# Causal attention tiles packed into full PSUM banks for two heads, with both causal passes moved to other slots

## The chip, the cores and the metric

The kernel runs on one core of one Trainium2 chip. The metric is the device time of the program in microseconds (us). All names of engines are those of the profile: PE is TensorE (PEld its weight loads), DVE is VectorE, ACT is ScalarE, POOL is GpSimd, SP is the engine that issues the DMA transfers.

## The reference

The input is 8 batches of 512 tokens of 128 numbers. One block of four parts runs over it, each after a layer norm and with a residual. In short:

```python
x = x + attn_a(layernorm(x))   # 16 heads of 8, causal, ALiBi:
#   scores = q @ k.T / sqrt(8) + where(k <= q, -(q - k), -1e30); softmax; @ v; @ w_out.T + b_out
x = x + ffn(layernorm(x))      # (silu(x @ wg.T) * (x @ wu.T)) @ wd.T, 384 hidden
x = x + attn_b(layernorm(x))   # full 512x512 softmax of each head only to rank tokens:
#   entropy, largest weight and influence choose 51 tokens; 64 compressed ones are added;
#   then attention of all queries over these 115 keys; @ Wo
x = x + ffn(layernorm(x))
```

Only attention a is touched by the change. Its scores are needed for pairs with k <= q alone: of the 4 by 4 squares of 128 by 128 in a head, ten, of which the four on the diagonal need a mask.

## The kernel before

**Slots.** Every engine's program is written as one loop over slots. A batch has its own count `a` of slots (`own_slots`), and a new batch starts every 64 slots (`NMAIN`), so that in the steady part one slot holds the work of up to four batches at different stages. What stands in a slot is set by constants: `A1_AT` (first causal pass), `A_TMAX`, `A_ROWS`, `A2_AT` (second causal pass), `A_TURN`, `A_GATE` and so on. I call a slot by its number `a` modulo 64. In each slot one "main tile" is worked as well, from slot `a` = 96 of the first batch on: one 128x512 tile of attention b. PE writes its scores one slot ahead (L1223) into a ring of three banks, DVE takes the maximum (L1045), ACT the exponential and its log sum (L811, L814), POOL a threshold (L680), DVE the entropy sum (L955, one slot later); PE adds four tiles' influence every fourth slot (L1231). Engines run their own program in order and wait only for semaphores.

**The first causal pass** (`causal_scores`, L1159 to L1164; `causal_maxima`, L916) finds the row maxima of each head. A head has three tiles (`CAUSAL`): query block 3 with 512 keys; blocks 0 and 2 with 128 and 384; block 1 with 256. Each block is one product, and then its diagonal square gets the mask by two more products of 64 columns each (L1162, L1164). The tiles alternate between banks 3 and 4, two a slot: 48 tiles, slots 0 to 23. DVE reduces each block one slot after it was written. Then the maxima are transposed (`A_TMAX` = 25, L1170), split into bf16 parts by ACT and POOL, and go through DRAM into rows of the query stack (`A_ROWS` = 28).

**The second pass** (`causal_minus_max`, L1181 to L1185) makes the scores again, keys on partitions, with the maximum taken off, again three tiles a head (`TILES`, widths 512, 512 and 256), two a slot, slots 32 to 55. ACT takes the exponential one slot later (L798) into `pT`. Heads go in gangs of four; when all four have a chunk, `weigh` (L1199) multiplies it with the values into bank 5. At the end of a gang ACT copies bank 5 out (`leave`, L781), PE transposes it into bank 7 (`turn_heads`, L1206, slots 40, 46, 52, 58) and DVE normalises (`norm_four`).

**Bank 7** is used by everything that is not one of these passes: a user claims it when the one before has been read (`claim`, by order of slots). In the slots that matter here it serves the feed-forward parts: of attention a's batch in slots 2 to 10 (gates in 2, 3, 4, silu in 5, ups in 6, 7, 8, down in 10), and of the batch three before in slots 43 to 51 (gates 43, 44, 45, silu 46, ups 48, 49, 50, down 51). ACT reads a gate in its own slot; DVE reads an up one slot later (`hidden`, L949).

**Layer norms** on POOL (L645, L652) stand in slots 24, 63, 12 and 35.

## Time and profile before

| | us |
|---|---|
| median of 3 runs | 1942.5 (1940.46 to 1942.92) |
| profiled execution | 1941.34, span 1939.2 |
| PE, DVE, ACT, POOL busy | 1524.0, 1224.2, 1006.8, 385.6 |
| first and last main tile (L1045) start | 245.3 and 1789.5 |
| one period (64 slots) in the middle | 209.6 |
| granted TensorE clock, mean | 0.687 of full speed |

Busy time is a union of the recorded times; the end of a matmul is modelled, so PE's is not what PE could not do without. The core is at work on five to six stages at once, so a share over the whole span says little; the period in the middle, cut where the change cuts, says more.

### The profile page before, as it was taken

To read this page: it belongs to the slowest core of one execution; us is meant where nothing else is said; L and a number is where in the kernel's file an instruction comes from. 1 tells how busy PE (TensorE), PEld (TensorE's weight loads), DVE (VectorE), ACT (ScalarE), POOL (GpSimd) and SP (SyncE) were. 2 spreads that over 40 slices of the span, in tenths; PEclk is the share of its full clock that TensorE was granted. 3 is DMA by queue.
4 is the path that set the end of the run, shared out by engine and by line. 5 is a ranking of instruction groups with operands and counts; after the bars stand their busy time and mean duration, and the time that the engine had idled before them with its cause. 6 is when DMAs were issued, how large, how long until landed. Compare 5 with 4: busy or idle time off the path is not lost.

```text
span 1939.2 us, 26667 instructions
## 1 busy us (share of the span) xinstructions
PE 1524.0 (79%) x8717; PEld 690.2 (36%) x8717; DVE 1224.2 (63%) x3259; ACT 1006.8 (52%) x2542; POOL 385.6 (20%) x900
## 2 busy tenths in 40 slices
PE   1687787878788888898889888788888878678655
PEld 1333443343344343353334343344334332321312
DVE  1503568866976577756876587757786667787211
ACT  1052276466556655656556655665565757546122
POOL 3110311320133011410133022310221012110100
PEclk9555588667766677668667786777666867665555
DMA  2110111121012110112012110221011002100000
GB/s 59 31 36 17 44 52 17 37 60 23 19 41 60 23 22 14 47 44 44 3 49 52 23 24 12 73 36 27 13 35 34 12 8 49 28 13 12 15 10 6
DMA packets 65626, 59.28 MB, mean 31 GB/s; under 512 B 11936, under 2 KB 63184, under 8 KB 65488
## 3 DMA queue, kind: packets, MB, share of 16 engines
q1 hardware_dynamic: 65488, 57.58, 13.3%
q8 instruction: 69, 1.13, 0.3%
q14 instruction: 69, 0.57, 0.1%
...
## 4 chain that ended last, share of the span: by engine, by line
PE 50%; DVE 23%; ACT 13%; issue 6%; POOL 5%; DMA 1%; ACTq 0%; SPq 0%; POOLq 0%; DVEq 0%
PE bank L1231 7%; PE bank L1271 7%; DVE nm L916 6%; DVE junk L955 5%; ACT setup L811 4%; PE bank L1223 4%; PE bank L1199 3%; PE bank L1254 3%; PE bank L1181 3%; PE bank L1159 3%; ACT pT L798 3%; DVE nmB L1045 3%; POOL xn L652 3%; DVE nm L923 2%; PE bank L1390 2%
## 5 line engine op out<-in xcount | busy, mean ns | idle before, releaser
L811 ACT ACTIVATE setup<-bank,nmB 128x512 f32<-128x512 f32 x512 | 350.3, 684 | 291.7 <-DVE nmB L1045 291.6
L955 DVE SCALAR_TENSOR_TENSOR junk<-bank,thr,setup 128x512 f32<-128x512 f32 x512 | 379.4, 741 | 84.8 <-POOL thr L680 81.5
L1045 DVE TENSOR_REDUCE nmB<-bank 128x1 f32<-128x512 f32 x512 | 351.2, 686 | 97.5 <-PE bank L1223 97.0
L1223 PE MATMUL bank<-k_stacks,q_stacks 48*128 48x512 bf16 x512 | 248.6, 487 | 135.5 <-DVE junk L955 133.1
L680 POOL TENSOR_TENSOR thr<-lnZ,nmB 128x1 f32<-128x1 f32 x512 | 96.5, 189 | 1223.5 <-ACT lnZ L814 1223.2
L916 DVE TENSOR_REDUCE nm<-bank 128x1 f32<-128x512 f32 (+3 forms) x512 | 223.7, 483 | 141.4 <-PE bank L1164 138.8
L798 ACT ACTIVATE pT<-bank 128x512 f32<-128x512 f32 (+1 forms) x384 | 184.1, 520 | 174.4 <-PE bank L1185 172.1
L1159 PE MATMUL bank<-k_stacks,q_stacks 52*128 52x512 bf16 (+3 forms) x512 | 177.1, 393 | 38.7 <-DMA k_stacks<-part_dram 17.7
L1231 PE MATMUL bank<-setup,rz 128*1 128x512 f32 x1024 | 196.6, 852 | 0.0
L1181 PE MATMUL bank<-q_stacks,k_stacks 55*128 55x384 bf16 (+3 forms) x512 | 159.2, 359 | 38.3 <-ACT pT L798 32.8
L1223 PEld LDWEIGHTS bank<-k_stacks,q_stacks 48*128 48x128 bf16 x512 | 49.5, 97 | 321.7 <-DVE junk L955 247.4
L1159 PEld LDWEIGHTS bank<-k_stacks,q_stacks 52*128 52x128 bf16 x512 | 54.5, 107 | 189.0 <-issue 121.8
L893 ACT ACTIVATE p<-bank 115x512 f32<-115x512 f32 x128 | 75.3, 588 | 87.3 <-PE bank L1390 87.0
L1199 PE MATMUL bank<-pT,vA 128*9 128x512 f32 (+3 forms) x1024 | 115.0, 554 | 1.0 <-ACT pT L798 1.0
L1162 PE MATMUL bank<-maskr,maskw 64*128 64x64 bf16 x512 | 114.6, 232 | 0.0
L1390 PE MATMUL bank<-s_stacks,kcst 51*115 51x512 bf16 x128 | 75.5, 590 | 49.4 <-ACT p L893 19.5
L814 ACT ACTIVATE lnZ<-Z 128x1 f32<-128x1 f32 x512 | 103.9, 203 | 16.2
L1164 PE MATMUL bank<-maskr,maskw 64*128 64x64 bf16 x512 | 109.0, 219 | 0.0
L1271 PE MATMUL bank<-xnT,wuT 128*128 128x512 f32 x96 | 81.8, 947 | 31.6 <-DVE gated L949 30.3
L1181 PEld LDWEIGHTS bank<-q_stacks,k_stacks 55*128 55x128 bf16 x512 | 52.7, 103 | 145.4 <-issue 81.5
L1183 PE MATMUL bank<-maskr,maskw 64*128 64x64 bf16 x512 | 104.2, 218 | 0.0
L811 ACT ACTIVATION_READ_ACCUMULATOR setup<-bank,nmB 128x1 f32 x512 | 102.2, 200 | 0.0
...
## 6 DMA issues: line engine op xcount, KB each, us to landing
...
q_stacks<-part_dram SPq DMA_DIRECT2D x192, 64.0 KB
k_stacks<-part_dram SPq DMA_DIRECT2D x192, 64.0 KB
...
```

The costliest lines, as they stand in the source:

```text
L798: act.activation(pT[h % HPQ][:, c * T:c * T + WIDTH[c]], bank[3 + u % 2][:, 0:WIDTH[c]], ACT.Exp).then_inc(s_free[3 + u % 2], 1)
L811: act.activation(E[:, n % NE, :], RING[n % RN][:, :], ACT.Exp, bias=nmB[mb % 2][:, h, t:t + 1], accum_out=Z[mb % 2][:, h, t:t + 1]).then_i ...
L916: last = dve.tensor_reduce(nm[0][:, t, h:h + 1], bank[k][:, at:at + (t + 1) * P], AX_X, ALU.max, negate=True)
L955: dve.scalar_tensor_tensor(out=junk[:, :], in0=RING[n % RN][:, :], scalar=thr[mb % 2][:, h, t:t + 1], in1=E[:, n % NE, :], op0=ALU.max, op ...
L1045: dve.tensor_reduce(nmB[mb % 2][:, h, t:t + 1], RING[n % RN][:, :], AX_X, ALU.max, negate=True).then_inc(s_bm, 1)
L1159: pe.matmul(bank[k][:, at:at + (t + 1) * P], qst[0][0:A_SC, h, t * P:(t + 1) * P], kst[0][0:A_SC, h, 0:(t + 1) * P], start=True, stop=True)
L1162: pe.matmul(bank[k][:, at + t * P:at + t * P + HF], maskw[:, 2, :], maskr[:, 2, :], start=False, stop=True, skip_group_check=True)
L1181: pe.matmul(bank[k][:, at:at + w], kst[0][0:A_MX, h, j * P:(j + 1) * P], qst[0][0:A_MX, h, j * P:T], start=True, stop=True)
L1199: last = pe.matmul(bank[5][QROWS * j:QROWS * j + HD + 1, k * P:T], vA[:, k, HPQ * g + j, :], pT[j][:, c * T + at:c * T + at + T - k * P], ...
L1223: pe.matmul(RING[n % RN][:, :], qst[1][0:B_SC, h, t * P:(t + 1) * P], kst[1][0:B_SC, h, :], start=True, stop=True).then_inc(s_bs, 1)
L1231: last = pe.matmul(INFL[QROWS * t:QROWS * t + 1, :], rz[mb % 2][:, h, t:t + 1], E[:, (NT * h + t) % NE, :], start=(h == 0), stop=(h == H - 1))
L1271: pe.matmul(bank[7][:, :], w, xnT[u][:, :], start=True, stop=True).then_inc(s_full[7], 1)
```

## The change

Both passes get tiles that fill a bank. In the first pass two heads share five tiles (`FIRST_TILES`): the four diagonal squares of one head, those of the other, blocks 3 and 1 below the diagonal (384 and 128 keys) of each, and block 2 (256) of both. The four diagonal squares are four products of 128 columns; their masks are two products of 4x64 columns. DVE takes the maxima of the diagonal squares in one instruction with four results, those of the other blocks into a second tile `nml`, and joins both with one minimum of negated maxima (a new instruction and a new semaphore `s_nm`). In the second pass the chunks of 256 of two heads share a tile, so that a gang has ten tiles and not twelve; squares of one bank share their masks. `pT` becomes one tensor, so that one exponential can write two heads.

A pass is 20 slots and not 24: the first in slots 8 to 27 (before 0 to 23), the second in 36 to 55 (before 32 to 55). What follows a pass moves with it: maxima transposed in 29 (25), rows in 32 (28), `weigh` in 38, 40, 41 and every five slots, turns in 43, 48, 53, 58 (40, 46, 52, 58). The next batch's preparation is two slots later (statistics 25, norm 26, transposes 28, q and k 30 and 31).

```diff
+    FIRST_TILES = (((0, None),), ((1, None),), ((0, 3), (0, 1)), ((1, 3), (1, 1)), ((0, 2), (1, 2)))
+    NF = len(FIRST_TILES)
     TILES = (((0, 0),), ((1, 0), (3, T - P)), ((2, 0),))
     WIDTH = (T, T, T - 2 * P)
-    CAUSAL = (((3, 0),), ((0, 0), (2, P)), ((1, 0),))
+    SHARE = (1, 1, 2)
...
+        pT = sb("pT", [P, 4, sum(WIDTH)])
         p2 = [sb(f"p2_{i}", [P, T]) for i in range(4)]
         ov = sb("ov", [P, T])
...
         INFL_LAG = 5
+        N1 = NF * H2
+        GANG = [(c, j) for c in range(3) for j in range(0, HPQ, SHARE[c])]
+        G2 = len(GANG)
+        N2 = G2 * NG
+        CHUNK_END = [max(i for i, (e, _) in enumerate(GANG) if e == c) for c in range(3)]
         LEAD = 1
-        FIRST = 44
-        X_LOAD = -44
-        P_STATS = -41
-        P_LN = -40
-        P_TURN = -38
-        P_Q, P_K = -36, -35
-        P_STORE = -30
-        P_HALF = (-20, -8)
+        FIRST = 42
+        X_LOAD = -42
+        P_STATS = -39
+        P_LN = -38
+        P_TURN = -36
+        P_Q, P_K = -34, -33
+        P_STORE = -28
+        P_HALF = (-17, -7)
         P_V = -4
-        A1_AT = 0
+        A1_AT = 8
         XBO = 19
-        A_TMAX = 25
-        A_ROWS = 28
-        A2_AT = 32
-        A_TURN = tuple(A2_AT + 8 + 6 * g for g in range(NG))
+        A_TMAX = 29
+        A_ROWS = 32
+        A2_AT = 36
+        A_TURN = tuple(A2_AT + 7 + 5 * g for g in range(NG))
+        WEIGH = tuple(A2_AT + 5 * g + (2, 4, 5)[c] for g in range(NG) for c in range(3))
         A_OUT = 60
         A_PROJ = 61
         A_LN = 63
...
-            for u in range(3 * H):
+            for u in range(N1):
                 use(3 + u % 2, z + A1_AT + u // 2, "a1", b, u)
+            for u in range(N2):
                 use(3 + u % 2, z + A2_AT + u // 2, "a2", b, u)
             use(3, z + A_TMAX, "tmax", b)
             for g in range(NG):
-                use(5, z + A2_AT + 2 + 6 * g, "weigh", b, g)
+                use(5, z + WEIGH[3 * g], "weigh", b, g)
                 use(7, z + A_TURN[g], "turn", b, g)
             use(7, z + A_OUT, "out", 0, b)
             use(7, z + A_PROJ, "proj", 0, b)
...
-            return HPQ * (u // (3 * HPQ)) + u % HPQ, u // HPQ % 3
+            c, j = GANG[u % G2]
+            return u // G2, c, range(j, j + SHARE[c])
         def own_slots(g):
...
+                        for u in range(N2):
                             if a == A2_AT + u // 2 + 1:
-                                h, c = gang_tile(u)
-                                if 3 * NG * b + u // HPQ > 2:
-                                    act.wait_ge(s_pv[0], 3 * NG * b + u // HPQ - 2)
+                                gang, c, js = gang_tile(u)
+                                if NG * b + gang:
+                                    act.wait_ge(s_pv[0], 3 * (NG * b + gang - 1) + c + 1)
                                 act.wait_ge(s_full[3 + u % 2], turn[3 + u % 2]["a2", b, u] + 1)
-                                act.activation(pT[h % HPQ][:, c * T:c * T + WIDTH[c]], bank[3 + u % 2][:, 0:WIDTH[c]],
+                                act.activation(pT[:, js[0]:js[0] + len(js), c * T:c * T + WIDTH[c]],
+                                               bank[3 + u % 2][:, :].rearrange("p (j q) -> p j q", j=len(js)),
                                                ACT.Exp).then_inc(s_free[3 + u % 2], 1)
                         for j in range(NG):
...
                 def causal_maxima(b, u):
-                    h, k = u // 3, 3 + u % 2
+                    k, blocks = 3 + u % 2, FIRST_TILES[u % NF]
+                    h = 2 * (u // NF) + blocks[0][0]
                     dve.wait_ge(s_full[k], turn[k]["a1", b, u] + 1)
-                    for t, at in CAUSAL[u % 3]:
-                        last = dve.tensor_reduce(nm[0][:, t, h:h + 1], bank[k][:, at:at + (t + 1) * P], AX_X, ALU.max,
-                                                 negate=True)
+                    if blocks[0][1] is None:
+                        last = dve.tensor_reduce(nm[0][:, :, h], bank[k][:, :].rearrange("p (t k) -> p t k", t=NT), AX_X,
+                                                 ALU.max, negate=True)
+                    elif blocks[0][1] == blocks[1][1]:
+                        last = dve.tensor_reduce(nml[:, 2, h:h + 2], bank[k][:, :].rearrange("p (j k) -> p j k", j=2), AX_X,
+                                                 ALU.max, negate=True)
+                    else:
+                        dve.tensor_reduce(nml[:, 3, h:h + 1], bank[k][:, 0:3 * P], AX_X, ALU.max, negate=True)
+                        last = dve.tensor_reduce(nml[:, 1, h:h + 1], bank[k][:, 3 * P:T], AX_X, ALU.max, negate=True)
                     last.then_inc(s_free[k], 1)
                 def small_maxima(b, h):
...
+                        for u in range(N1):
                             if a == A1_AT + u // 2 + 1:
                                 causal_maxima(b, u)
+                        if a == A_TMAX - 1:
+                            dve.wait_ge(s_free[3], turn[3]["a1", b, N1 - 2] + 1)
+                            dve.wait_ge(s_free[4], turn[4]["a1", b, N1 - 1] + 1)
+                            dve.tensor_tensor(nm[0][:, 1:NT, :], nm[0][:, 1:NT, :], nml[:, 1:NT, :], ALU.min
+                                              ).then_inc(s_nm, 1)
                         for h in range(H):
                             if a == S1_AT + h // 2 + 1:
                                 small_maxima(b, h)
...
                 def causal_scores(b, u):
-                    h, k = u // 3, 3 + u % 2
+                    k = 3 + u % 2
                     claim(k, "a1", b, u)
-                    if u in (0, 3 * H2):
-                        pe.wait_ge(s_stack[0][u // (3 * H2)], 2 * NPAIR * DMA * (b + 1))
-                    for t, at in CAUSAL[u % 3]:
-                        pe.matmul(bank[k][:, at:at + (t + 1) * P],
-                                  qst[0][0:A_SC, h, t * P:(t + 1) * P], kst[0][0:A_SC, h, 0:(t + 1) * P],
-                                  start=True, stop=True)
-                        pe.matmul(bank[k][:, at + t * P:at + t * P + HF], maskw[:, 2, :], maskr[:, 2, :],
-                                  start=False, stop=True, skip_group_check=True)
-                        last = pe.matmul(bank[k][:, at + t * P + HF:at + (t + 1) * P], maskw[:, 3, :], maskr[:, 3, :],
-                                         start=False, stop=True, skip_group_check=True)
+                    if u in (0, N1 // 2):
+                        pe.wait_ge(s_stack[0][2 * u // N1], 2 * NPAIR * DMA * (b + 1))
+                    at = 0
+                    for j, t in FIRST_TILES[u % NF]:
+                        h = 2 * (u // NF) + j
+                        if t is None:
+                            for t in range(NT):
+                                here = slice(t * P, (t + 1) * P)
+                                pe.matmul(bank[k][:, here], qst[0][0:A_SC, h, here], kst[0][0:A_SC, h, here],
+                                          start=(t == 0), stop=True, skip_group_check=(t > 0))
+                            halves = bank[k][:, :].rearrange("p (t c k) -> p t c k", t=NT, c=2)
+                            for c in range(2):
+                                last = pe.matmul(halves[:, :, c, :], maskw[:, 2 + c, :],
+                                                 maskr[:, 2 + c:3 + c, :].broadcast_to([HF, NT, HF]), start=False,
+                                                 stop=True, skip_group_check=True)
+                        else:
+                            last = pe.matmul(bank[k][:, at:at + t * P], qst[0][0:A_SC, h, t * P:(t + 1) * P],
+                                             kst[0][0:A_SC, h, 0:t * P], start=True, stop=True)
+                            at += t * P
                     last.then_inc(s_full[k], 1)
                 def transpose_max(s, ps):
...
                 def causal_minus_max(b, u):
-                    h, c = gang_tile(u)
+                    g, c, js = gang_tile(u)
                     k = 3 + u % 2
                     claim(k, "a2", b, u)
                     if u == 0:
                         pe.wait_ge(s_mrow[0], DMA * (b + 1))
-                    for j, at in TILES[c]:
-                        w = T - j * P
-                        pe.matmul(bank[k][:, at:at + w], kst[0][0:A_MX, h, j * P:(j + 1) * P],
-                                  qst[0][0:A_MX, h, j * P:T], start=True, stop=True)
-                        pe.matmul(bank[k][:, at:at + HF], maskw[:, 0, :], maskr[:, 0, :],
-                                  start=False, stop=True, skip_group_check=True)
-                        last = pe.matmul(bank[k][:, at + HF:at + P], maskw[:, 1, :], maskr[:, 1, :],
-                                         start=False, stop=True, skip_group_check=True)
+                    squares = []
+                    for i, head in enumerate(js):
+                        h = HPQ * g + head
+                        for j, at in TILES[c]:
+                            w, first = T - j * P, i * WIDTH[c] + at
+                            pe.matmul(bank[k][:, first:first + w], kst[0][0:A_MX, h, j * P:(j + 1) * P],
+                                      qst[0][0:A_MX, h, j * P:T], start=not squares, stop=True,
+                                      skip_group_check=bool(squares))
+                            squares.append(first // P)
+                    blocks = bank[k][:, :].rearrange("p (t c q) -> p t c q", t=NT, c=2)
+                    step = squares[-1] - squares[0] or 1
+                    for half in range(2):
+                        last = pe.matmul(blocks[:, squares[0]:squares[-1] + 1:step, half, :], maskw[:, half, :],
+                                         maskr[:, half:half + 1, :].broadcast_to([HF, len(squares), HF]), start=False,
+                                         stop=True, skip_group_check=True)
                     last.then_inc(s_full[k], 1)
                 def weigh(b, w):
                     g, c = w // 3, w % 3
-                    u = HPQ * w + HPQ - 1
-                    pe.wait_ge(s_free[3 + u % 2], turn[3 + u % 2]["a2", b, u] + 1)
+                    for u in (g * G2 + CHUNK_END[c] - 1, g * G2 + CHUNK_END[c]):
+                        pe.wait_ge(s_free[3 + u % 2], turn[3 + u % 2]["a2", b, u] + 1)
                     if c == 0:
                         claim(5, "weigh", b, g)
                     if w == 0:
...
-                            pe.wait_ge(s_free[4], turn[4]["a1", b, 3 * H - 1] + 1)
+                            pe.wait_ge(s_nm, b + 1)
                             transpose_max(0, bank[3]).then_inc(s_full[3], 1)
                         for j in range(NG):
                             if a == A_TURN[j]:
```


PE, the first tiles of the first causal pass at the program's start: before, one head is twelve products in three tiles.

```order
L1159 MATMUL bank3<-k_stacks,q_stacks 128x512
L1162 MATMUL bank3<-maskr,maskw 128x64
L1164 MATMUL bank3<-maskr,maskw 128x64
L1159 MATMUL bank4<-k_stacks,q_stacks 128x128
L1162 MATMUL bank4<-maskr,maskw 128x64
L1164 MATMUL bank4<-maskr,maskw 128x64
L1159 MATMUL bank4<-k_stacks,q_stacks 128x384
L1162 MATMUL bank4<-maskr,maskw 128x64
L1164 MATMUL bank4<-maskr,maskw 128x64
L1159 MATMUL bank3<-k_stacks,q_stacks 128x256
L1162 MATMUL bank3<-maskr,maskw 128x64
L1164 MATMUL bank3<-maskr,maskw 128x64
```


Now two heads are five tiles (the four products of a row with x4 are the diagonal squares of one head).

```order
L1192 MATMUL bank3<-k_stacks,q_stacks 128x128 x4
L1196 MATMUL bank3<-maskr,maskw 128x4x64 x2
L1192 MATMUL bank4<-k_stacks,q_stacks 128x128 x4
L1196 MATMUL bank4<-maskr,maskw 128x4x64 x2
L1200 MATMUL bank3<-k_stacks,q_stacks 128x384
L1200 MATMUL bank3<-k_stacks,q_stacks 128x128
L1200 MATMUL bank4<-k_stacks,q_stacks 128x384
L1200 MATMUL bank4<-k_stacks,q_stacks 128x128
L1200 MATMUL bank3<-k_stacks,q_stacks 128x256 x2
```


The masks went from eight products a head to two, the blocks from four to seven; the columns are the same.

PE, where a feed-forward part and the second pass meet (batches three and later): before, slot 45 with the last gate, and the start of slot 46. L1223 is the main tile's product, L1271 a gate, L1231 the influence, L1206 the turn.

```order
L1223 MATMUL bank1<-k_stacks,q_stacks 128x512
L1271 MATMUL bank7<-xnT1,wgT 128x512
L1231 MATMUL bank6<-setup,rz0 1x512 x4
L1181 MATMUL bank3<-q_stacks,k_stacks 128x512
L1183 MATMUL bank3<-maskr,maskw 128x64
L1185 MATMUL bank3<-maskr,maskw 128x64
L1181 MATMUL bank4<-q_stacks,k_stacks 128x512
L1183 MATMUL bank4<-maskr,maskw 128x64
L1185 MATMUL bank4<-maskr,maskw 128x64
L1223 MATMUL bank2<-k_stacks,q_stacks 128x512
L1206 MATMUL bank7<-identf,ov 128x128 x4
```


Now, slot 43 with the first gate, and the start of slot 44. L1268 is the main tile's product, L1316 a gate, L1251 the turn, L1221 and L1229 are the second pass, L1244 is `weigh`.

```order
L1268 MATMUL bank1<-k_stacks,q_stacks 128x512
L1316 MATMUL bank7<-xnT1,wgT 128x512
L1251 MATMUL bank7<-identf,ov 128x128 x4
L1221 MATMUL bank3<-q_stacks,k_stacks 128x384
L1221 MATMUL bank3<-q_stacks,k_stacks 128x128
L1229 MATMUL bank3<-maskr,maskw 128x2x64 x2
L1221 MATMUL bank4<-q_stacks,k_stacks 128x384
L1221 MATMUL bank4<-q_stacks,k_stacks 128x128
L1229 MATMUL bank4<-maskr,maskw 128x2x64 x2
L1244 MATMUL bank5<-pT,vA 9x512 x4
L1268 MATMUL bank2<-k_stacks,q_stacks 128x512
L1316 MATMUL bank7<-xnT1,wgT 128x512
```


The turn used to stand in the slot after the last gate. It now follows the first gate directly, and both write bank 7; in slot 48 it follows the first up (wuT) in the same way.

## Rows read from the trace of the kernel before

**Rows 1.** The page: busy time by engine, and the chain that ended last, by engine

```profile
PE 1524.0 (79%) x8717; PEld 690.2 (36%) x8717; DVE 1224.2 (63%) x3259; ACT 1006.8 (52%) x2542; POOL 385.6 (20%) x900
...
PE 50%; DVE 23%; ACT 13%; issue 6%; POOL 5%; DMA 1%; ACTq 0%; SPq 0%; POOLq 0%; DVEq 0%
```

**Rows 2.** Stretches of one period: length, busy PE, PEld, DVE, ACT, POOL, PEclk, DMA

```profile
1148.00:1170.20 22.20, 18.55 (x99) 7.07 (x99) 19.95 (x51) 15.73 (x34) 7.52 (x15) 0.81 0.02 5
1170.20:1227.50 57.30, 47.57 (x270) 21.52 (x269) 45.16 (x120) 28.67 (x73) 15.40 (x33) 0.65 0.14 42
1227.50:1239.00 11.50, 9.22 (x42) 3.25 (x42) 9.04 (x26) 6.33 (x17) 5.94 (x10) 0.69 0.00 0
1239.00:1250.00 11.00, 9.23 (x26) 1.65 (x26) 6.36 (x18) 10.16 (x26) 3.78 (x7) 0.69 0.06 17
1040.40:1057.50 17.10, 16.74 (x113) 10.26 (x112) 11.33 (x38) 9.98 (x26) 3.97 (x10) 0.69 0.53 113
1057.50:1125.80 68.30, 58.95 (x421) 27.36 (x418) 38.77 (x112) 43.55 (x112) 8.20 (x26) 0.78 0.13 24
1125.80:1148.00 22.20, 16.18 (x120) 9.07 (x120) 21.17 (x58) 9.70 (x31) 2.03 (x11) 0.80 0.21 37
```

**Rows 3.** Groups of instructions by form: a mask product (busy us, mean ns)

```profile
L1162 PE MATMUL bank<-maskr,maskw 64*128 64x64 bf16 x512 | 114.6, 232 | 0.0
```

**Rows 4.** Timeline of PE (start us, us): mask products, clock low, then full

```profile
1149.64 0.26 PE L1162 MATMUL bank<-maskr,maskw 64*128 64x64 bf16 x1
1149.71 0.24 PE L1164 MATMUL bank<-maskr,maskw 64*128 64x64 bf16 x1
...
1163.98 0.19 PE L1162 MATMUL bank<-maskr,maskw 64*128 64x64 bf16 x1
1164.01 0.19 PE L1164 MATMUL bank<-maskr,maskw 64*128 64x64 bf16 x1
```

**Rows 5.** Timeline of DVE: statistics; a full tile, three smaller reductions, what follows

```profile
1225.70 0.86 DVE L905 BATCH_NORM_STATS2 st<-x 128x6 f32<-128x128 f32 x4
1226.60 0.38 DVE L909 BATCH_NORM_AGGREGATE mv<-st 128x2 f32<-128x6 f32 x4
...
1227.54 0.68 DVE L1045 TENSOR_REDUCE nmB<-bank 128x1 f32<-128x512 f32 x1
1228.14 1.07 DVE L916 TENSOR_REDUCE nm<-bank 128x1 f32<-128x128 f32 x3
1229.13 0.16 DVE L1058 RECIPROCAL rz<-Z 128x4 f32<-128x4 f32 x1
```

**Rows 6.** Timelines of POOL, PE, DVE and ACT: slots 0 to 5 of the period

```profile
1148.96 3.13 POOL L652 TENSOR_SCALAR xn<-x,mv,rstd 128x128 f32<-128x128 f32 x4
...
1155.33 0.60 PE L1223 MATMUL bank<-k_stacks,q_stacks 48*128 48x512 bf16 x1
...
1157.41 0.69 DVE L1045 TENSOR_REDUCE nmB<-bank 128x1 f32<-128x512 f32 x1
...
1165.31 1.48 ACT L785 ACTIVATE gated<-gated 128x1536 f32<-128x1536 f32 x1
```

**Rows 7.** Timelines: bank 7 in slots 43, 46 and 48 (PE, ACT, DVE)

```profile
1087.51 1.13 PE L1271 MATMUL bank<-xnT,wgT 128*128 128x512 f32 x2
...
1094.59 0.66 PE L1206 MATMUL bank<-identf,ov 128*128 128x128 f32 x4
...
1102.66 2.07 PE L1271 MATMUL bank<-xnT,wuT 128*128 128x512 f32 x2
...
1088.68 0.60 ACT L727 ACTIVATE gated<-bank 128x512 f32<-128x512 f32 x1 [0.44 <-PE bank L1271]
...
1104.77 0.69 DVE L949 TENSOR_TENSOR gated<-bank,gated 128x512 f32<-128x512 f32 x1 [0.44 <-PE bank L1271]
```

**Rows 8.** Stretches of the start, same columns: the first two passes alone

```profile
55.00:90.40 35.40, 29.44 (x192) 16.12 (x190) 27.64 (x69) 0.00 (x0) 0.00 (x0) 0.50 0.14 22
105.00:158.20 53.20, 49.43 (x330) 21.25 (x330) 1.92 (x8) 26.09 (x52) 1.11 (x2) 0.50 0.16 37
```

14 lines of the change are left out of this document (7 added, 7 removed).

## The prediction

> **What bounds the kernel now.** I read the page first. PE is recorded busy for 1524.0 of 1939.2 us and is half of the chain that ended last, with DVE at 23% [rows 1]. That does not say which pass waits for what, so I cut one period in the middle at the starts of main tiles, where the change cuts [rows 2]. In order these are slots 0 to 7, 8 to 23, 24 to 27, 28 to 31, then (from the start of the same period) 32 to 35, 36 to 55 and 56 to 63. The reader is to compare each length with the busy time of each engine. Slots 0 to 7, which hold a feed-forward part beside the first pass, are DVE's (19.95 of 22.20). Slots 8 to 23 are nobody's alone (PE 47.57, DVE 45.16 of 57.30). Slots 28 to 31 are ACT's (10.16 of 11.00). Slots 32 to 35 are PE's (16.74 of 17.10). Slots 36 to 55 are mostly PE's (58.95 of 68.30), and 56 to 63 DVE's. So both passes run in stretches where they cost time, and the question is what their work costs in the new place against the old one.
>
> **The masks.** 2048 mask products become 896: 8 to 2 a head in the first pass, 32 to 20 a gang in the second. The page gives one of them 232 ns [rows 3]. That is its way through the array, not what it costs: the next product starts 0.07 us after it at the low clock and 0.03 us at the full one [rows 4]. 64 columns at 1.2 and 2.4 GHz are 0.053 and 0.027, so PE pays for columns, and the columns are the same before and after (1792 a head and pass). What goes is the rest of 0.003 to 0.017 a product: 1152 fewer masks and 384 more block products are 768 instructions, at most 13 us of PE over the whole program if all are at the upper end, some 4 us at 0.005. PE is the limit in little more than half of the time and PE's other gaps swallow part of it: I take 0 to 5 us, and none in the sum.
>
> **DVE.** A full tile keeps the next instruction away for 0.60 us. Three reductions of 768 columns together take 0.99 [rows 5]. Two equations give 0.067 + 0.00104 a column. One reduction of seven (two heads had eight) is 0.067 x 64 = 4.3 us saved over eight batches, less eight joins of 48 numbers (estimated 0.12 each). For a slot it gives the old load 853 columns and 2.67 reductions, 1.065 us; the new load is 1024 and 2.8, 1.25 us. The Trainium skill ("VectorE: DVE Perf Modes", the TRN2 errata) has a fixed 120 cycles for a PSUM source, 0.125 us at 0.96 GHz. By it the saving would be 8 us; the rows show half of that from start to start.
>
> **ACT.** A gang had eight full and four half tiles, and has ten full ones: the same columns, two instructions fewer. I give that nothing, as ACT's own queue bounds few slots.
>
> **The first pass moves from slots 0-23 to 8-27.** Six batches do this beside main tiles.
> *Slots 0 to 7.* POOL's norm ends at 1152.09, whatever DVE does, so slots 63 to 1 give back nothing. The next main product on PE is at 1155.33, and DVE could take its maximum at about 1155.9, but takes it at 1157.41, after the first pass's tile [rows 6]: 1.5 back. From there three gates at 1.85 each (PE 1.13, ACT 0.60 to read it [rows 7], 0.12 of hand-over, an estimate) bring silu's activation to about 1162.5 where it is at 1165.31 now [rows 6]: 2.8 back. The first `hidden` behind it no longer stands behind a slot's reductions and their main tile's work on DVE (1.25 and 1.27): up to 2.4 more. Together at most some 5.2, if the clock is full for all of it. The stretch's granted clock is 0.81 [rows 2]. If the gates run at the low one, each costs 2.07 [rows 7] and 2.5 is left. I take 4.0.
> *Slots 8 to 23.* DVE gets 16 x 0.185 = 2.96, less slot 8 (no tile is ready yet, 1.06) and less the statistics of the next batch, which leave for slot 25 (1.1 [rows 5]): 0.8. PE gets 0.133 head a slot, 16 x 0.133 x 1792 columns, 3.2 us at 1.2 GHz and 2.4 at the granted 0.65. Between these: 1.5 lost.
> *Slots 24 to 27.* DVE has 9.04 of 11.50. It gets 4 x 1.25, less 1.06 of slot 24, plus 1.1: 14.1. That is 2.6 over the present length before any stall, and 5.1 if all of the present 2.5 of idle stays. 3.0 lost.
> *Slots 28 to 31.* The transposes and bf16 parts of the maxima come in (three ACT copies like the one of 0.60 in [rows 7], on 10.16 of 11.00; two copies of the next batch's parts go out), and q now follows the maxima by one slot where it had three. 0 to 2.5 lost, 1.3 taken.
> Net 1.8 lost a batch, 10.8 for six.
>
> **The second pass moves from 32-55 to 36-55.** Slots 32 to 35 lose eight tiles of PE work, 5632 columns, 4.7 us at 1.2 GHz, and one `weigh` of 1.8; at the granted 0.69 that is 4.7, and PE is the limit there. ACT and DVE then stand near: 4.3 gained. Slots 36 to 55 get the same 6.5 us of low-clock work back; at 0.78 it is 4.2 us, of which 86% is where PE is busy, and slots that are ACT's pay for 8 more half tiles. 3.5 lost. Net 0.8 gained, seven batches: 5.6.
>
> **A wait that is new.** The turn needs bank 7. In slot 43 it now stands behind the first gate, and so waits until ACT has read it; in slot 48 behind the first up, until DVE has. Today PE goes on with second-pass tiles in that time. The gate starts at 1087.51 and is read by 1089.2; the up starts at 1102.66, ends at 1104.73 and is read by 1105.4 [rows 7]. PE stands 0.6 to 0.8 each time, with the tiles and the `weigh` of the slot queued behind, and ACT's exponentials behind these. 1.6 a batch for the five batches where both meet: 8.0. Bound: 0 if PE would wait for ACT in these slots anyway, 3 a batch if ACT falls a slot behind. The turn itself (0.66) only moves.
>
> **The start.** Batch 0's passes run alone. The first takes 35.40 for 16 heads, of which DVE is busy 27.64, 0.48 a head of waiting for three tiles; two and a half tiles and half a reduction less give back 0.11 a head, 1.8. The second takes 53.2 for four gangs at clock 0.50 [rows 8]; its 12288 columns a gang fill 41.0 of them at 1.2 GHz (a float32 column of `weigh` counted four times, an estimate from the 2.07 of the up in [rows 7]), so 12 hand-overs cost 3.0 a gang, and ten give back 0.5, 2.0 in all. Batch 1's first pass has its first eight slots hidden under a feed-forward part today and will have three: 2.5 lost. Sum 1.3 gained.
>
> **Sum.** 10.8 - 5.6 + 8.0 - 1.3 = 11.9 us more, on the profiled 1941.34, which is 1.2 below the median of 1942.5: 1953.2, or 1954.4 against the median. I keep back 2 for the masks and the DVE instruction: 1952.
>
> **Rivals.**
> *The dense slots swallow the work (faster, 0.31).* Slots 8 to 31 have 79.8 us against 60.6 of DVE, and 36 to 55 have 9 us without PE. If the added work falls into those gaps, the lower ends hold: -5.2 + 0.8 + 2.6 + 0 = -1.8 for six, -4.7 + 2.0 = -2.7 for seven, and half of the bank-7 wait: -10.8 - 18.9 + 4 - 1.3 = -27, 1915. Half of that is 1928. It decides if slots 24 to 27 grow by under 3 and slots 0 to 7 shrink by over 4.
> *The clock (slower, 0.10).* In 1148.0 to 1170.2 the granted share is 0.81. Without the first pass PE has gaps there: if it stays at 1.2 GHz through the three gates and three ups, these cost 0.94 more each, 5.6 a batch, and 12 + 34 gives up to 1985; half of it is 1970.
> *The masks are on the path (faster, 0.05).* If each product waited for the one before to leave the array, a removed mask would be worth its recorded 0.232 [rows 3]: 1152 x 0.232 = 267 us off PE, half of it on the chain [rows 1], 1808. The starts in [rows 4] speak against it. The Trainium skill ("TensorE: Matmul & The Clock Gate", single matmul latency) gives an isolated product (219 + N)/1.2 ns, 236 for 64 columns; by that rule alone the saving would be this rival's.
> *Nothing (0.12).* The terms have both signs and may cancel: 1939 to 1946.
>
> **How the numbers follow.** The forecast, slower by the sum, has 0.42, its own range is 1947 to 1970. A measurement of this kernel tells 0.2% (4 us) from no change. Slower has 0.40 + 0.10 = 0.50, the same 0.12 + 0.02 of the forecast = 0.14, faster 0.31 + 0.05 = 0.36. The range 1915 to 1978 leaves out the masks' case, the ends of the first two rivals, together under 0.2.
>
> **What would show it.** Right: slots 0 to 7 take about 18 us in the new trace, slots 24 to 27 above 14 with DVE full, 32 to 35 about 13; PE idles before the turn (L1251) behind an ACT or DVE read of bank 7 some ten times by 0.6 to 0.8; mask products start 0.21 us apart at the low clock where they are 4x64. PE's recorded busy time falls by far more than the span moves. Wrong: slots 8 to 31 no longer than now, a PE clock well off 0.687, or the maxima rows late at slot 36 (SP now issues the next half stack right behind them).

## The result, and the profile after

| | before | after |
|---|---|---|
| median of 18 runs each, us | 1941.24 (1935.53 to 1952.88) | 1929.83 (1910.79 to 1943.08) |
| span and granted clock of the profiled execution | 1939.2, 0.687 | 1928.7, 0.692 |

The ratio is 0.9926, with a 95% interval of 0.9901 to 0.9951. The change makes the kernel faster, by 11 us, where I forecast 12 us slower. 1929.83 lies inside the range of 1915 to 1978, on the other side of the kernel before.

The page of after, busy time by engine and the chain by engine (as [rows 1] of before):

```profile
PE 1487.1 (77%) x7949; PEld 652.0 (34%) x7949; DVE 1223.3 (63%) x3203; ACT 1001.2 (52%) x2478; POOL 389.4 (20%) x900
...
PE 50%; DVE 22%; ACT 15%; issue 7%; POOL 3%; DMA 2%; SPq 0%; ACTq 0%; POOLq 0%; DVEq 0%
```

768 products fewer, as worked out. DVE's time has not moved: seven reductions for two heads are a little longer each than eight were. The chain's shares are nearly the same too.

The middle period of after, cut at the same slots as [rows 2] (0 to 7, 8 to 23, 24 to 27, 28 to 31, then from the start of that period 32 to 35, 36 to 55, 56 to 63). Columns: length, busy PE, PEld, DVE, ACT, POOL, granted clock, DMA:

```profile
1135.20:1155.30 20.10, 14.55 (x42) 3.74 (x42) 12.81 (x32) 15.45 (x34) 7.54 (x15) 0.75 0.02 5
1155.30:1209.60 54.30, 45.08 (x251) 20.60 (x252) 45.59 (x112) 28.19 (x73) 15.39 (x33) 0.69 0.17 41
1209.60:1223.90 14.30, 11.82 (x63) 4.25 (x61) 13.97 (x42) 6.93 (x19) 4.87 (x10) 0.62 0.08 15
1223.90:1234.00 10.10, 8.75 (x36) 2.31 (x34) 7.55 (x21) 7.94 (x20) 1.83 (x6) 0.63 0.00 0
1022.40:1038.60 16.20, 13.32 (x78) 8.52 (x78) 12.05 (x34) 10.31 (x26) 10.42 (x15) 0.73 0.39 102
1038.60:1110.60 72.00, 59.93 (x388) 27.44 (x388) 38.97 (x112) 44.76 (x109) 5.71 (x23) 0.78 0.17 31
1110.60:1135.20 24.60, 19.40 (x141) 10.52 (x140) 21.37 (x58) 10.63 (x31) 2.02 (x11) 0.73 0.20 33
```

Length against the forecast for it:

| slots | before | after | difference | forecast |
|---|---|---|---|---|
| 0 to 7 | 22.2 | 20.1 | -2.1 | -4.0 |
| 8 to 23 | 57.3 | 54.3 | -3.0 | +1.5 |
| 24 to 27 | 11.5 | 14.3 | +2.8 | +3.0 |
| 28 to 31 | 11.0 | 10.1 | -0.9 | +1.3 |
| 32 to 35 | 17.1 | 16.2 | -0.9 | -4.3 |
| 36 to 55 | 68.3 | 72.0 | +3.7 | +3.5, and 1.6 of the wait |
| 56 to 63 | 22.2 | 24.6 | +2.4 | 0 |

This period grew by 2.0. But it was one of the shortest of before: four of its periods in a row, counted from slot 0, take 212.9, 217.7, 211.3 and 209.1 (the period of the table, cut at slot 32, takes 209.6). So I take four whole periods of each (first row before, then after), with the columns as above:

```profile
506.10:1357.10 851.00, 718.37 (x4353) 329.59 (x4352) 607.50 (x1627) 499.92 (x1264) 187.27 (x433) 0.72 0.15 34
```

```profile
499.80:1346.80 847.00, 691.70 (x3969) 309.43 (x3968) 609.09 (x1599) 497.12 (x1232) 191.17 (x433) 0.73 0.16 34
```

Four periods gain 4.0 us, 1.0 each. Of their stretches, slots 8 to 23 change most: their mean is 58.3 us before, at clock 0.63, and 54.4 after, at 0.69. Length times clock, which is microseconds of full clock, is 36.8 before and 37.5 after: the columns that moved in are there, and the stretch is shorter all the same, because the clock is higher.

The start gains more. The first main tile stands at 245.3 before and at 230.2 after, 15.1 earlier; but where the four periods begin (506.1 and 499.8) only 6.3 of it is left. What follows the four periods takes 582.1 and 581.9. So the 10.5 us between the two spans are 6.3 and 4.0, and 0.2 behind. The start in after: the first pass alone, and the second pass alone in two parts (as [rows 8]):

```profile
55.20:88.00 32.80, 28.22 (x140) 12.65 (x138) 27.25 (x62) 0.00 (x0) 3.22 (x5) 0.50 0.13 22
101.20:125.00 23.80, 23.33 (x140) 9.44 (x141) 0.55 (x2) 12.77 (x23) 0.00 (x0) 0.50 0.13 44
125.00:138.80 13.80, 12.64 (x126) 6.10 (x122) 1.10 (x4) 10.53 (x20) 0.00 (x0) 0.99 0.26 41
```

From first to last exponential the second pass took 50.0 before, all at clock 0.50, and takes 37.6. The last third now runs at the full clock.

**The view that orders the rest.** The granted clock has two levels, 1.2 GHz (0.5) and 2.4 GHz (1.0), and a mean between them is a share of both. If PE always had work, the span times the mean granted clock would be the work itself in microseconds of full clock, whatever the clock did; a wait adds to it. PE is recorded busy for 77 to 79% of the span, so the product counts work and idle time together. The table has the mean of span x clock over the executions of each kernel, without six that took over 1.5% more than the fastest of their kernel (one each of the change, first_at_4, prep_new, second_alone, before_shared and after_two; that of prep_new took 2639.06 us):

| kernel | executions | span, mean | clock, mean | product |
|---|---|---|---|---|
| before | 93 | 1939.5 | 0.6878 | 1334 |
| the change | 21 | 1924.3 | 0.6921 | 1332 |
| places_old | 12 | 1949.7 | 0.6821 | 1330 |
| first_alone | 12 | 1942.0 | 0.6882 | 1336 |
| second_alone | 11 | 1937.1 | 0.6916 | 1340 |
| prep_new | 9 | 1948.5 | 0.6874 | 1340 |
| first_at_4 | 9 | 1931.7 | 0.6957 | 1344 |
| first_unpacked_late | 12 | 1934.2 | 0.6913 | 1337 |
| turn_apart, turn_again | 10 | 1925.7 | 0.6867 | 1322 |
| first_masks_pairs | 10 | 1926.0 | 0.6909 | 1331 |
| first_masks_apart | 4 | 1963.0 | 0.6790 | 1333 |
| masks_apart | 6 | 1967.2 | 0.6817 | 1341 |
| before_shared | 10 | 1931.4 | 0.6919 | 1336 |
| before_two | 4 | 679.8 | 0.5932 | 403 |
| after_two | 4 | 664.8 | 0.6042 | 402 |

Before and the change have nearly the same product, and so have their periods: the four above take 153.3 and 153.7 us of full clock each. The change is faster by about what its clock is higher: 0.6% of clock, 0.8% of time. Within one kernel, too, the quick executions are those with the higher clock (correlation -0.81 over the 93 of before, -0.86 over the 21 of the change). This says where the time went, and not what raised the clock.

### The profile page after: what moved, and what is told of

Same layout as the page of the kernel before. It is cut to its first block, busy times and chain, and to the rows that moved or that the text cites. A ratio compares the mean times of both kernels' runs of the same rounds, so it can differ in the third digit from the quotient of the medians.

```text
span 1928.7 us, 25028 instructions
## 1 busy us (share of the span) xinstructions
PE 1487.1 (77%) x7949; PEld 652.0 (34%) x7949; DVE 1223.3 (63%) x3203; ACT 1001.2 (52%) x2478; POOL 389.4 (20%) x900
## 4 chain that ended last, share of the span: by engine, by line
PE 50%; DVE 22%; ACT 15%; issue 7%; POOL 3%; DMA 2%; SPq 0%; ACTq 0%; POOLq 0%; DVEq 0%
PE bank L1276 8%; PE bank L1316 7%; DVE junk L978 5%; ACT setup L827 4%; PE bank L1268 4%; PE bank L1244 3%; PE bank L1221 3%; PE bank L1299 3%; DVE nm L946 3%; ACT pT L813 2%; DVE nmB L1068 2%; DVE nm L933 2%; PE bank L1259 2%; PE bank L1251 2%; PE bank L1200 2%
## 5 line engine op out<-in xcount | busy, mean ns | idle before, releaser
L1268 PE MATMUL bank<-k_stacks,q_stacks 48*128 48x512 bf16 x512 | 254.5, 499 | 151.8 <-DVE junk L978 150.1
L813 ACT ACTIVATE pT<-bank 128x512 f32<-128x512 f32 x320 | 174.3, 590 | 133.5 <-PE bank L1229 132.1
L1268 PEld LDWEIGHTS bank<-k_stacks,q_stacks 48*128 48x128 bf16 x512 | 49.9, 98 | 384.2 <-DVE junk L978 285.3
L1221 PE MATMUL bank<-q_stacks,k_stacks 55*128 55x384 bf16 (+3 forms) x512 | 138.9, 346 | 36.6 <-ACT pT L813 30.7
L933 DVE TENSOR_REDUCE nm<-bank 128x4 f32<-128x512 f32 x128 | 86.5, 687 | 65.8 <-PE bank L1196 65.8
L1200 PE MATMUL bank<-k_stacks,q_stacks 52*128 52x384 bf16 (+2 forms) x384 | 96.0, 364 | 12.9 <-DVE nm L933 9.6
L1244 PE MATMUL bank<-pT,vA 128*9 128x512 f32 (+3 forms) x1024 | 104.9, 511 | 0.2 <-ACT pT L813 0.2
L1316 PE MATMUL bank<-xnT,wuT 128*128 128x512 f32 x96 | 83.0, 961 | 25.8 <-DVE gated L972 23.8
L667 POOL TENSOR_SCALAR xn<-x,mv,rstd 128x128 f32<-128x128 f32 x128 | 100.1, 794 | 3.3
L1229 PE MATMUL bank<-maskr,maskw 64*128 64x128 bf16 (+1 forms) x640 | 91.4, 227 | 0.0
L1192 PE MATMUL bank<-k_stacks,q_stacks 52*128 52x128 bf16 x512 | 68.4, 275 | 29.3 <-DMA k_stacks<-part_dram 17.3
L956 DVE RECIPROCAL rzo<-bank 128x16 f32<-128x16 f32 x64 | 15.7, 245 | 113.0 <-PE bank L1251 113.0
L946 DVE TENSOR_REDUCE nm<-bank 128x4 f32<-128x460 f32 x128 | 74.9, 629 | 16.2 <-PE bank L1310 15.8
```

Source lines behind the costliest of these rows:

```text
L813: act.activation(pT[:, js[0]:js[0] + len(js), c * T:c * T + WIDTH[c]], bank[3 + u % 2][:, :].rearrange("p (j q) -> p j q", j=len(js)), ACT ...
L933: last = dve.tensor_reduce(nm[0][:, :, h], bank[k][:, :].rearrange("p (t k) -> p t k", t=NT), AX_X, ALU.max, negate=True)
L946: dve.tensor_reduce(nm[1][:, :, h], bank[k][:, 0:NT * NK].rearrange("p (t k) -> p t k", t=NT), AX_X, ALU.max, negate=True).then_inc(s_free ...
L1200: last = pe.matmul(bank[k][:, at:at + t * P], qst[0][0:A_SC, h, t * P:(t + 1) * P], kst[0][0:A_SC, h, 0:t * P], start=True, stop=True)
L1221: pe.matmul(bank[k][:, first:first + w], kst[0][0:A_MX, h, j * P:(j + 1) * P], qst[0][0:A_MX, h, j * P:T], start=not squares, stop=True, s ...
L1244: last = pe.matmul(bank[5][QROWS * j:QROWS * j + HD + 1, k * P:T], vA[:, k, HPQ * g + j, :], pT[:, j, c * T + at:c * T + at + T - k * P], ...
```

## The experiments

### Which part gains: packing, or the places

```diff
 # places_old: the change, with
-A1_AT, A_TMAX, A_ROWS, A2_AT = 8, 29, 32, 36    # and P_*, FIRST of the change
+A1_AT, A_TMAX, A_ROWS, A2_AT = 4, 25, 28, 32    # and P_*, FIRST of before
 # first_alone: first pass packed, slots 4 to 23; second pass and preparation as before
 # second_alone: second pass packed, slots 36 to 55; first pass as before, slots 0 to 23
```

> All tiles packed as in the change, but every stage near its old slot: the first pass in slots 4 to 23, the maxima at 25, the second pass in 32 to 51, the next batch's preparation as before. If the gain comes of the packing alone (fewer hand-overs, shorter passes), this is as fast as the change, some 1925 to 1932. If it comes of where the passes stand (first pass out of the feed-forward slots 0 to 7), half of slots 0 to 7 is loaded again and this is 5 to 15 us slower than the change, 1935 to 1945. The turns in 39, 44, 49, 54 meet gates and ups in two slots here too.

> Only the first causal pass is packed (20 slots, 4 to 23); the second is the old one in 32 to 55. If the steady gain is the first pass's (slots 0 to 15 were 5.4 us shorter a period in the changed trace, the second pass's slots 5 us longer), this is faster than the change: 1905 to 1925. If the gain is that of the second pass at the start (full clock for half of it), this is near the kernel before, 1935 to 1942.

> Only the second causal pass is packed (36 to 55); the first is the old one in 0 to 23. If the second pass costs in the steady part (about 5 us a period in the two traces), this is slower than the kernel before, 1945 to 1975, less what the start gives. If the start's second pass at the full clock is the gain, this is 1925 to 1935.

Measured: places_old 1952.59 us (12 runs), ratio 1.0045 [1.0022, 1.0068]; first_alone 1945.13 (12), 1.0005 [0.9983, 1.0027]; second_alone 1944.28 (12), 0.9987 [0.9962, 1.0012]. Packing at the old places loses, and neither pass alone gains. Tiles and places together do. The expectations did less well: places_old is over 7 us above both of its cases, and first_alone 3 us above "near the kernel before". For second_alone the first case holds: four of its periods take 861.3 us for 851.0 before, and the time stands at the low end of 1945 to 1975.

### Where the new places count

```diff
 # first_unpacked_late: the change, first pass with the three tiles of before, slots 4 to 27
 # first_at_4: the change, with
-A1_AT = 8
+A1_AT = 4
 # prep_new: places_old, with the preparation (P_*, FIRST) of the change
```

> The change, but with the old three tiles a head in the first pass, which stands in slots 4 to 27 (the second pass packed in 36 to 55, all else as in the change). If the steady gain comes of the first pass's end being later and its work out of the feed-forward slots, half of those slots is loaded again: slots 0 to 15 take some 50 us in a period, between the 47.6 of the change and the 53.0 of before, and the time is 1935 to 1942. If it came of fewer, fuller tiles, slots 8 to 27 are longer here as well and the time is above 1942. If neither matters, 1930.

> The change, with the first pass alone four slots earlier (slots 4 to 23 in place of 8 to 27), so that its first four slots stand beside the feed-forward products of slots 0 to 7; maxima, rows, second pass and preparation stay. Theory that the second pass's place and not the first's made the packed kernel with old places slow (there slots 32 to 63 took 118.4 us a period against 112.7 in the change, slots 0 to 31 only 100.2 against 98.8): 1.4 us a period more, 1936 to 1942 us. Rival, that the first pass must keep off the feed-forward slots: most of the 22.8 us between the two, 1945 to 1952 us. Second rival: its place doesn't count, 1928 to 1932 us.

> The packed tiles with both passes and the maxima at their old places (first pass 4 to 23, second pass 32 to 51), and the preparation of the next batch at its new ones; so it stands between places_old (1952.6 us, preparation old as well) and first_at_4 (1934.7 us, second pass at 36). Theory that the second pass's place counts, in whose stretch places_old took 118.4 us a period against 112.7: 1948 to 1956 us. Rival, that the preparation's place counts (its q and k products and transposes stood beside the last first-pass slots): 1933 to 1940 us.

Measured: first_unpacked_late 1934.67 (12 runs), 0.9971 [0.9949, 0.9993]; first_at_4 1934.73 (10), 0.9979 [0.9950, 1.0008]; prep_new 1948.27 (10), 1.0055 [1.0031, 1.0079]. With the tiles packed, the 22.8 us between old and new places are 4.3 for the preparation (1952.6 to 1948.3), 13.5 for the second pass at 36 in place of 32, the maxima moving with it (to 1934.7), and 4.9 for the first pass at 8 in place of 4 (to 1929.8). The first is within its error, the last is about as large as its error, and the middle one is well clear of it. Its sign is that of the clock: prep_new has 0.6874 and first_at_4 0.6957, at products of 1340 and 1344. Of the expectations, that of prep_new holds. first_at_4 lies between two of its cases.

first_unpacked_late has the old first pass with its 1024 masks of 64 columns, and still gains about 6 of the 11 us. So packing the first pass is not all of the gain, once the passes stand later. Its time and its slots 0 to 15 (48.1 and 49.6 us in turn) are close to what its first case had (1935 us or more, some 50).

### The new wait on bank 7

```diff
-A_TURN = tuple(A2_AT + 7 + 5 * g for g in range(NG))   # 43, 48, 53, 58
+A_TURN = (46, 52, 53, 58)
+A_LEAVE = tuple(A2_AT + 6 + 5 * g for g in range(NG))  # ACT's copy stays in its slot
```

> The change with the copy out of bank 5 kept where it is and the turns in slots 46, 52, 53, 58, so that no turn stands behind a gate or an up in its own slot. If the new wait for bank 7 costs the 1.6 us a batch that was forecast, in five batches, this is 8 us faster than the change, about 1922. If PE would have waited for ACT there anyway, it is the same within 3 us.

> The change with the turns at slots 46, 52, 53 and 58 and the leaves where they were, a second time. Theory that it takes 2 us a period out of slots 40 to 55 whatever the clock does (span times clock in slots 40 to 55 42.9 us there against 44.9 in the change), so that it lies 8 to 16 us under the change at the same start: 1915 to 1922 us, with a profile under 1915 us if its start gets the full clock. Rival, that the clock gives back what the wait had cost: 1925 to 1931 us again.

What the turn's products wait for, in the change, and then in turn_apart (idle time of PE before them in us, and times; weight loads left out):

```profile
its engine sat idle before it (us, times) until:
  ACT gated L742: 11.2, 5
  ACT ov L796: 6.5, 14
  DVE gated L972: 5.0, 5
```

```profile
its engine sat idle before it (us, times) until:
  ACT ov L797: 7.1, 17
  DVE o L959: 0.6, 1
```

The rows for the gate and the up (L742, L972) are gone. They were 2.2 us a batch for the gate and 1.0 for the up, in five batches. Slots 40 to 55 of the middle period, the change and then turn_again:

```profile
1053.80:1110.60 56.80, 48.41 (x320) 21.23 (x320) 27.28 (x65) 36.37 (x88) 3.56 (x17) 0.79 0.12 24
```

```profile
1062.30:1115.40 53.10, 47.98 (x320) 20.81 (x320) 27.01 (x65) 36.24 (x88) 3.55 (x17) 0.81 0.13 26
```

3.7 us a period, in both profiles of this version. Yet its times are 1927.74 (6 runs, ratio 0.9921 [0.9891, 0.9951]) and 1929.73 (4 runs, 0.9945 [0.9929, 0.9961]), those of the change. Its product is 10 lower, 1322, and its clock also, 0.687 for 0.692. turn_apart is not the 8 us faster that the wait should have been worth, and within 3 us of the change. Of the expectation for the second run the rival holds, in the time. The traces show where the gain is lost again, and it is not in the periods. Four whole periods of turn_apart, the same length as in turn_again:

```profile
517.50:1350.20 832.70, 689.91 (x3969) 307.75 (x3968) 608.51 (x1597) 496.88 (x1232) 191.92 (x433) 0.73 0.16 35
```

They are 14.3 us shorter than the 847.0 of the change, but they begin at 517.5 and 515.5 where those of the change begin at 499.8. The first batch's second pass ran at clock 0.54 there and at 0.68 in the change, and the slots 40 to 55 just before the four periods took 45.8 and 45.9 us at 0.66 and 0.67 where the change has 37.1 at 0.91. Why this version gets less clock there is not shown.

### The masks

```diff
 # masks_apart: both passes; first_masks_apart: first pass alone
-for c in range(2):
-    last = pe.matmul(halves[:, :, c, :], maskw[:, 2 + c, :], maskr[:, 2 + c:3 + c, :].broadcast_to([HF, NT, HF]), ...)
+for t in range(NT):
+    for c in range(2):
+        last = pe.matmul(halves[:, t, c, :], maskw[:, 2 + c, :], maskr[:, 2 + c, :], ...)
 # first_masks_pairs: halves[:, t:t + 2, c, :], two squares in a product
 # before_shared: before, its tiles and places kept; where a bank holds two squares, both
 # blocks first and then two mask products of 128 columns in place of four of 64
```

> The change with the masks not shared: every diagonal square gets its two products of 64 columns again (2048 mask products, not 896), the tiles and slots as in the change. If a mask product costs its columns (0.03 to 0.07 us from start to start), this is within 5 us of the change, 1927 to 1936. If it costs the recorded 0.23 us on the path, this is 60 us or more slower, above 1990.

> The change, with the mask products of the first pass's diagonal squares alone issued one by one (1024 of 64 columns where the change has 256 of 256 columns); the second pass keeps its 640 shared ones. Theory that the unshared masks cost granted clock in the stretch where the first pass runs: with all masks apart, slots 8 to 23 of a period took 30.5 and 29.1 us at a granted clock of 0.61 and 0.62, where the change takes 27.5 and 26.8 at 0.69, while the 64-column products start 53 ns and the 256-column ones 213 ns apart, the same time for a column. So nearly the whole 39 us should stand here: 1960 to 1972 us, ratio 1.010 to 1.016 against before, slots 8 to 31 about 6 us a period longer than in the change, and slots 32 to 63 as in the change. Rival, a fixed price of each further product (39 us over 1152 products, 34 ns each): 768 more products here, 1956 us, and starts further apart than 53 ns. Second rival, that the second pass's masks are what counts: within 5 us of the change, 1930 to 1935 us.

> The change with the first pass's mask products for two squares at a time: 512 of 128 columns, where the change has 256 of 256 and the kernel with them apart 1024 of 64; the columns are the same in all three. Theory that the granted clock falls with the count of short products in the first pass's stretch: a third of the way from 1930 to 1963 us, 1937 to 1945 us, with a clock of 0.65 to 0.68 in slots 8 to 23. Rival, a step as soon as the products are shorter than 256 columns: 1955 to 1965 us. Second rival, a step only at 64 columns: 1928 to 1933 us.

> The kernel before, its tiles, banks and places unchanged; only where a bank holds two diagonal squares (one tile of three in each pass) both blocks are computed first and their masks issued together, 128 columns each: 1024 products of 64 columns and 512 of 128 in place of 2048 of 64. Theory that 64-column masks hold the granted clock down in the kernel before as in the packed one (34 us for 1024 such products in the first pass against 256 or 512 longer ones): half of them gone, 1922 to 1933 us, ratio 0.990 to 0.996, with a clock over 0.65 in slots 8 to 23. Rival, that the price stands only where the squares of a whole head follow one another, as in the packed first pass: within 3 us of before, 1938 to 1944 us.

| | mask products and their columns | us | ratio to before |
|---|---|---|---|
| masks_apart | 2048 of 64 | 1969.10 (6 runs) | 1.0137 [1.0106, 1.0168] |
| first_masks_apart | first pass 1024 of 64 | 1963.43 (4) | 1.0129 [1.0079, 1.0178] |
| first_masks_pairs | first pass 512 of 128 | 1930.27 (10) | 0.9935 [0.9905, 0.9965] |
| before_shared | 1024 of 64, 512 of 128 | 1940.23 (11) | 0.9960 [0.9930, 0.9990] |

masks_apart lies between its two cases. Splitting the first pass's masks into 64 columns costs 34 us, as first_masks_apart had it; splitting them into 128 costs nothing, the second rival of first_masks_pairs. A fixed price for each product is out, as the 256 further products of the pairs would then have cost 11 us. The products themselves are no dearer either. A head's masks on PE at the low and at the full clock (start, us), masks_apart and then the change:

```profile
1193.76 0.63 PE L1197 MATMUL bank<-maskr,maskw 64*128 64x64 bf16 x8
...
1204.08 0.40 PE L1197 MATMUL bank<-maskr,maskw 64*128 64x64 bf16 x8
```

```profile
1159.07 0.63 PE L1196 MATMUL bank<-maskr,maskw 64*128 64x256 bf16 x2
...
1194.00 0.38 PE L1196 MATMUL bank<-maskr,maskw 64*128 64x256 bf16 x2
```

Eight products or two, 0.63 at the low clock and 0.40 or 0.38 at the full one. What differs is the clock that is granted around them. Slots 8 to 15 and 16 to 23 of one period, first_masks_apart, first_masks_pairs, and the change in a second profile (below):

```profile
1169.20:1199.60 30.40, 26.81 (x162) 13.29 (x162) 23.17 (x62) 12.18 (x32) 5.93 (x15) 0.61 0.06 18
1199.60:1228.60 29.00, 24.86 (x168) 11.73 (x168) 22.56 (x53) 16.01 (x41) 9.54 (x18) 0.62 0.25 56
```

```profile
1162.90:1190.50 27.60, 23.54 (x138) 10.75 (x138) 23.07 (x60) 12.18 (x32) 5.90 (x15) 0.69 0.07 20
1190.50:1214.40 23.90, 19.54 (x140) 9.31 (x140) 22.42 (x53) 15.76 (x41) 9.53 (x18) 0.79 0.30 64
```

```profile
1139.90:1167.40 27.50, 23.32 (x126) 10.23 (x126) 23.02 (x60) 12.18 (x32) 5.94 (x15) 0.69 0.07 20
1167.40:1191.30 23.90, 19.35 (x126) 8.79 (x126) 22.42 (x53) 15.76 (x41) 9.56 (x18) 0.79 0.30 65
```

30.4 x 0.61 is 18.5 and 27.5 x 0.69 is 19.0: no more work in microseconds of full clock, only a lower clock. The Trainium skill ("TensorE: Matmul & The Clock Gate", back-to-back issue gap) gives a start-to-start gap of the columns at the clock, plus 2.5 ns at the full one. The traces agree for a product: 64-column masks of masks_apart start 53 ns apart at the low clock and 28 or 29 at the full one, 256-column masks of the change 213 and 113. By that rule the 1152 products of masks_apart would cost under 3 us in all, an estimate; 39 are measured.

Nor do 64-column masks hold the clock down wherever they stand. first_unpacked_late has as many of them in its first pass as first_masks_apart, in the old tiles, and takes 1934.67 us; its slots 8 to 15 and 16 to 23 had the clock 0.70 and 0.79 in two of four periods (0.67 and 0.62 in the other two). So the 34 us are the price of these masks in the packed first pass.

In the kernel before the price shows in some executions only. before_shared lies 0.4% under it, near the edge of what its interval can tell, and its median missed the expected 1922 to 1933. But all but one of its times fall into two groups, five of 1921 to 1931 (clock 0.694 to 0.697) and five of 1940 to 1943 (0.688 to 0.689), and none of the 93 executions of before is under 1934.33. Its profiled execution took 1925.49. Four of its periods:

```profile
511.70:1344.50 832.80, 695.71 (x4096) 312.63 (x4096) 607.06 (x1627) 498.19 (x1264) 187.14 (x433) 0.74 0.16 35
```

That is 18.2 us less than the 851.0 of before, and in two of the four periods slots 8 to 15 and 16 to 23 have the clock 0.68 and 0.70, as its theory had it. So longer masks alone, with no packed tile and no pass moved, can give as much as the whole change, in half of the executions. What decides which execution gets it is open.

### Start or steady part

```diff
 # before_two, after_two: before and the change, with
+B = 2
 # after_again: the change itself once more
```

> The kernel before, for the first two batches alone (the other six outputs are not written): the start, two periods and the end. With the start's second pass at the low clock in every execution its times should lie close together, some 650 to 700 us, spread under 5.

> The change for the first two batches alone, to be read against the kernel before for two. If the start's gain is the clock rising in the second pass in some executions, its times spread by 10 us or more and the median is 5 to 12 us below. If the start gains by its fewer hand-overs alone, it is 1 to 4 us below with a small spread. If all of the gain is in the steady periods, it is the same.

> The change itself once more, for a second profile of it. Theory that the start's stretch of full clock (the second pass of the first batch 37.6 us, of it 12.3 and 7.7 us a gang at the low and at the full clock) comes in only some of its executions, and that a time goes with the share of the clock that was granted: a profile near the median (1927 to 1933 us) with this pass at 37 to 43 or at 45 us, whichever, and span times mean clock at 1330 to 1336 us, as in the first profile (1928.7 x 0.692 = 1334.7) and in before (1939.2 x 0.687 = 1332.2). Rival, that the start is always as in the first profile: 37 to 38 us again and the first main tile at 230 us.

before_two and after_two compute two of the eight batches and leave the other six outputs unwritten. They took 680.15 us (4 runs, 679.80 to 685.87) and 667.57 us (5 runs, 663.31 to 681.52). So two batches show a gain of 12.6, as large as eight do, and their product is nearly the same too (403 and 402). That speaks for the start as the source of the gain in the median, but does not settle it: the profiles of before and of the change with eight batches keep 6.3 us of the start, and the second profile of the change, below, gains more in its periods. The spread of before_two is 6.1, three of its four times lying within 0.5 of each other; that of after_two is 18, with one time of 681.52.

after_again took 1922.36 (4 runs), 0.9892 [0.9857, 0.9927]; its profiled execution is the fastest of all, span 1906.6 at clock 0.701. Its start is that of the first profile, as the rival had it: second pass 37.7 us, first main tile at 231.2. Its four periods take 833.3 for 847.0:

```profile
494.70:1328.00 833.30, 681.45 (x3969) 303.03 (x3968) 608.17 (x1599) 495.90 (x1232) 191.87 (x433) 0.74 0.17 35
```

The difference lies in slots 16 to 23, which run at 0.79 in 23.9 us (the row above) where the first profile has 0.69 in 26.8; all other stretches of eight slots agree within 0.4. Each of these two executions keeps its pattern from period to period (208.3 and 211.6 us). That is not so in every version: the four periods of before go from 209.1 to 217.7. Is the start always so? Not in all versions of it: the packed second pass took 45.4 at clock 0.50 in the profiles of masks_apart, places_old and second_alone, 44.7 and 44.8 at 0.54 in turn_apart and turn_again, 42 at 0.57 in four others, and 33 to 38 at 0.68 or more in four. The unpacked one took 50.0 at 0.50 in all four profiles.

## Why the prediction was wrong, point by point

- **Slots 8 to 23, +1.5.** The step that failed by most, as it stands in the sum six times. It came to -3.0 in the period of the table, and over four periods to -3.9 in the first profile of the change and -6.8 in the second (58.3 to 54.4 and 51.5). The step added the columns that move in and divided them by the present clock of 0.65. The columns did come (36.8 us of full clock before, 37.5 and 37.7 after), but at a clock of 0.69 or 0.73 in place of 0.63.
- **The start, -1.3.** -6.3 where the four periods begin, and -15.1 at the first main tile. The first pass gave 2.6 (35.4 to 32.8) where I had 1.8. For the second I had 2.0 for fewer hand-overs. Packing alone gives 4.6 (50.0 to 45.4, both at clock 0.50), and a stretch of full clock takes 3 to 12 more in some profiles. I had worked out PE's time at 1.2 GHz as if that clock were given; that it may rise was in no term and no rival.
- **Slots 24 to 27, +3.0**, and DVE full: right, +2.8 with DVE 13.97 of 14.30.
- **Slots 0 to 7, -4.0**: mis-sized, -2.1; the clock fell from 0.81 to 0.75. The clock rival had a falling clock in this stretch; the fall is a small part of its size, and over the whole kernel the clock rose.
- **Slots 32 to 35, -4.3**: mis-sized, -0.9. I took out the second pass's PE time, and PE is busy for 13.32 of 16.20 now, so the stretch is no longer PE's. DVE has as much to do as before (12.05 for 11.33), and POOL has 10.42 for 3.97, as the bf16 parts of the next batch's q and k come in with the later preparation. Which of them keeps the stretch long is not shown.
- **Slots 28 to 31, +1.3**: wrong sign, -0.9. ACT was to get more work there and has less, 7.94 busy for 10.16. **Slots 56 to 63** had no term; they grew by 0.9 over the four periods (2.4 in the period of the table).
- **The bank-7 wait, 1.6 a batch**: the mechanism was right, in the place and for the reason given; but it is 2.2 for the gate and 1.0 for the up where I had 0.8 each. In slot 43 ACT has main-tile work and second-pass exponentials ahead of the gate: the gate ends at 1066.72 and is read from 1068.33 on. Taken away, the wait moves 3.7 us a period in the trace and nothing in the median.
- **The masks, 0 to 5 and none in the sum.** The cost of a product was read rightly. What failed is the step from there to the time: in the packed first pass 64-column masks cost 34 us through the clock. Without shared masks the change would be slower than before by 1.4%, the sign that I forecast.
- **The sum.** It was made for one period, and that one was 3.1 under the mean of four in before (209.6 against 212.7). Two slips move nothing: the two equations for DVE give 0.060 + 0.00105 a column and so a saving of 3.8 and not 4.3, and the clock rival's 1985 adds to the span; the time would be 1987.
- **The signs.** Of those for "right", slots 24 to 27, the wait before the turn, the mask starts 0.21 us apart and PE's busy time (36.9 less, the span 10.5) came true; slots 0 to 7 at 18 and 32 to 35 at 13 did not. Of those for "wrong", slots 8 to 31 are no longer than before (78.7 for 79.8).

The rival nearest to what happened, "the dense slots swallow the work", gave 1915 to 1928, with the right sign (slots 8 to 31 together do not grow), but as far as the product of span and clock tells, for another reason: had the work fallen into gaps, the product would be smaller, and it is nearly unchanged.

Shown: with about the same product of span and clock, the time is lower by what the clock is higher; the gain needs masks of 128 columns or more in the packed first pass, and the second pass at 36; two batches alone already show a gain as large. Not shown is what raises the clock. Open: why short masks lower it in the packed first pass, in half of the executions of the kernel before, and not in first_unpacked_late; why the second pass at 32 does; how much of the change's gain is that of the shared masks alone, for no run shares all of them at the old tiles and places; and whether turn_apart misses the better pattern by chance. No version beats the change beyond its error.
